# Relation products ahead of a block's sums, one-hots behind the messages, and an own order for the last set's products

## The reference, cut to what matters

```python
def _gat(x, W, asrc, adst, b, src, dst):
    h = (x @ W).reshape(n, HEADS, HID)                 # 4 heads of 64
    es = jnp.sum(h * asrc, axis=-1); ed = jnp.sum(h * adst, axis=-1)
    e = jax.nn.leaky_relu(es[src] + ed[dst], 0.2)
    emax = jax.ops.segment_max(e, dst, num_segments=n)
    ex = jnp.exp(e - emax[dst])
    den = jax.ops.segment_sum(ex, dst, num_segments=n)
    out = jax.ops.segment_sum(h[src] * (ex / den[dst])[:, :, None], dst, num_segments=n)
    return out.mean(axis=1) + b
# layer 1, layer 2, each with a layer norm and relu; then h @ Wo + bo, added to x, layer norm
# relational layer:
out = x @ W0
h = jnp.einsum('nd,rdo->rno', x, W)                    # 8 relations
msg = h[edge_type, src] * edge_weight[:, None]
out = (out + jax.ops.segment_sum(msg, dst, num_segments=num_nodes)) / deg[:, None]
```

## Time and profile before

| what | value |
|---|---|
| median of 3 runs | 3734.32 us (3734.08 to 3737.24) |
| the profiled execution, whole | 3735.32 us |
| its span in the profile | 3733.7 us |
| POOL busy | 1742.3 us (47%) |
| DVE busy | 2104.0 us (56%) |
| PE busy | 2435.0 us (65%) |
| ACT busy | 729.1 us (20%) |

### The profile page before, as it was taken

The page is one execution under the profiler, slowest core; times in us unless marked ns, Lnnn a source line. Parts: engine busy times, 40 slices in busy tenths (PEclk is TensorE's granted clock), DMA queues, the critical chain, the costliest instruction groups (busy, mean ns, idle before and its releaser), DMA issues.

```text
span 3733.7 us, 49457 instructions
## 1 busy us (share of the span) xinstructions
PE 2435.0 (65%) x14591; PEld 1745.1 (47%) x14592; DVE 2104.0 (56%) x5733; ACT 729.1 (20%) x1115; POOL 1742.3 (47%) x1837
## 2 busy tenths in 40 slices
PE   5879999999999945565535666662333344545556
PEld 3545666666666534444424444442323233444444
DVE  8985555555555636666646666662333233555555
ACT  5870000000000033322222333320000002222222
POOL 2220000000000067777747777725777776777771
PEclk9989999999999967777767777776666666677778
DMA  2000000000000064444434555532222223444441
GB/s 66 5 1 0 0 0 0 0 0 0 0 0 0 13 180 138 137 142 140 121 112 132 154 154 155 151 88 59 58 58 59 58 61 106 131 131 131 130 124 44
DMA packets 139378, 283.87 MB, mean 76 GB/s; under 512 B 35751, under 2 KB 79123, under 8 KB 139155
## 3 DMA queue, kind: packets, MB, share of 16 engines
q0 software_dynamic: 77760, 204.68, 19.9%
q1 hardware_dynamic: 24603, 53.25, 4.3%
q10 hardware_dynamic: 36864, 24.07, 2.2%
HBM read 255.10 MB, written 27.01 MB: 76 GB/s over the span
## 4 chain that ended last, share of the span: by engine, by line
POOL 31%; issue 11%; DVE 10%; PE 10%; DMA 2%; ACT 1%; ACTq 0%; POOLq 0%; DVEq 0%
POOL t_rows L1833 11%; POOL t_rows L2176 11%; POOL t_rows L2497 9%; PE t_sum_ps L1930 5%; DVE t_onehot L1761 2%; PE t_product_ps L1650 1%; DVE t_rows L2009 1%; DVE t_stage L2577 1%; PE t_sum_ps L2548 1%; DMA t_rows<-gat_table,t_src 1%; DMA t_rows<-kv_table_b,t_src 1%; DVE t_stage L2572 1%; PE t_small_ps L1900 0%; DVE t_so_far L1984 0%; ACT t_stage L1687 0%
## 5 line engine op out<-in xcount | busy, mean ns | idle before, releaser
L1038 PE MATMUL hop_ps<-parts,counts 128*128 128x384 bf16 (+1 forms) x6150 | 1003.3, 326 | 2.2 <-DVE parts L1099 2.2
L1833 POOL DMA_INDIRECT t_rows<-gat_table,t_src x880 | 838.4, 953 | 323.2 <-issue 264.1
L1038 PEld LDWEIGHTS hop_ps<-parts,counts 128*128 (+1 forms) x6150 | 603.4, 98 | 402.2 <-issue 10.2
L1930 PE MATMUL t_sum_ps<-t_rows,t_onehot 128*128 128x264 f32 x1760 | 511.3, 460 | 229.1 <-DVE t_rows L2009 229.0
L1930 PEld LDWEIGHTS t_sum_ps<-t_rows,t_onehot 128*128 128x128 f32 x1760 | 404.1, 233 | 319.8 <-issue 213.7
L2176 POOL DMA_INDIRECT t_rows<-rel_table_b,t_rel x440 | 417.9, 950 | 211.6 <-issue 133.2
L2497 POOL DMA_INDIRECT t_rows<-kv_table_b,t_src x440 | 416.4, 946 | 153.0 <-issue 131.9
L1464 POOL IOTA t_node<- 128x1 f32 x1 | 0.1, 131 | 1044.6 <-POOLq L106 1044.6
L2194 PE MATMUL t_sum_ps<-t_rows,t_onehot 128*128 128x128 f32 x880 | 159.1, 365 | 332.9 <-DMA t_rows<-rel_table_b,t_rel 332.9
L2194 PEld LDWEIGHTS t_sum_ps<-t_rows,t_onehot 128*128 128x128 f32 x880 | 155.1, 278 | 341.2 <-issue 341.2
L2527 PE MATMUL t_small_ps<-t_own,t_turned 128*128 128x128 bf16 x1032 | 118.5, 311 | 246.0 <-DVE t_stage L2572 240.4
(11 more groups left out here) (351 smaller groups left out, 2873.0 us busy)
## 6 DMA issues: line engine op xcount, KB each, us to landing
t_dst_wide<-dst_row SPq DMA_DIRECT2D x72, 576.0 KB, 4.3
t_rows<-gat_table,t_src POOLq DMA_INDIRECT x880
rel_table_b<-t_stage ACTq DMA_DIRECT2D x25, 512.0 KB, 3.6
t_rows<-rel_table_b,t_rel POOLq DMA_INDIRECT x440, 2.5
t_rows<-kv_table_b,t_src POOLq DMA_INDIRECT x440, 2.7
gat_table<-t_own ACTq DMA_DIRECT2D x10, 520.0 KB, 4.7
kv_table_b<-t_fresh ACTq DMA_DIRECT2D x5, 512.0 KB, 3.0
out<-x SPq DMA_DIRECT2D x6, 256.0 KB
```

The lines of the kernel that those rows point to most:

```text
L1038: last = nc.tensor.matmul(ps[bank][0:m, 0:PARTS * D], counts[:, k, columns], parts[old][:, k, :], start=(k == 0), stop=(k == NB - 1))
L1833: c.nc.gpsimd.indirect_dma_start(t.rows[:, slot(k), 0:FW], None, self.table, bass.IndirectOffsetOnAxis(ap=t.src[:, k:k + 1], axis=0)).then ...
L1930: product = c.nc.tensor.matmul(t.pa[b % 2][:, 0:RW], t.onehot[:, hot_at(k), :], t.rows[:, slot(k), :], start=(n == 0), stop=(n == len(ks) ...
```

## The change

Four edits:

1. **PE and ACT, in each block of both layers' loop:** `late(b)`, the relation products of two blocks, stands before the block's own sums on PE (behind `look_up`), and on ACT directly behind the block's exponentials, before `own_weight` and `turn`. Behind layer 1 `late` does nothing.
2. **DVE, both layers:** `make_hots(b + 1)` moves from before `messages(b)` to behind `close(b - 1)` and the norm, and `view(b + 1)` moves with it, ahead of `self.after.dve`. For block 23 (y) the one-hots of block 24 move behind `close(x)`.
3. **The last set's products** (`pe_last`, `act_last`, `dve_last`): the 512-column products of a block go to PSUM bank 0 and 1, ACT copies the first half out and DVE the second, and the DMA of the block goes out after both. The three W0 products (128 columns) follow after all six halves.
4. **Relational layer:** since the last W0 products are copied out late, PE waits for them before its first sums (`own_out`), and DVE before it closes block 22.

No instruction is added or taken away but for three copies that change engine, three DMAs that stay on ACT, and waits.

```diff
--- before.py
+++ after.py
@@ -1603,6 +1603,15 @@
     def act_late(self, act, i, blocks):
         pass
 
+    def pe_last(self, pe):
+        pass
+
+    def act_last(self, act):
+        pass
+
+    def dve_last(self, dve):
+        pass
+
     def dve(self, dve, layer, i):
         dve.wait_ge(self.out, SETS[i][-1] + 1)
         then = chained(dve, self.step, 4 * i)
@@ -1619,6 +1628,7 @@
         self.early, self.late = 0, 0
         self.turned, self.copied, self.done, self.added, self.normed, self.step, self.x_turned, self.x_copied, self.x_done, self.x_out = (
             c.sem(f"into_rel_{n}") for n in ("turned", "copied", "products", "added", "normed", "step", "x_turned", "x_copied", "x_products", "x_out"))
+        self.x_out_dve = c.sem("into_rel_x_out_dve")
         self.tabled = [c.sem(f"into_rel_tabled{q}") for q in range(3)]
 
     def pe(self, pe, layer, i):
@@ -1648,6 +1658,54 @@
                 if k >= 2:
                     pe.wait_ge(self.x_out, k - 1)
                 c.nc.tensor.matmul(t.pr[k % 2][:, 0:(hi - lo) * D], t.turned_all[:, j * P:(j + 1) * P], t.w_rel[:, lo:hi, :], start=True, stop=True).then_inc(self.x_done, 1)
+
+    def pe_last(self, pe):
+        c, t, blocks = self.c, self.t, SETS[-1]
+        n, k0 = len(blocks), 3 * blocks[0]
+        self.pe_turn(pe, len(SETS) - 1)
+        for j in range(n):
+            columns = t.turned_all[:, j * P:(j + 1) * P]
+            pe.wait_ge(self.x_out, k0 + j - (j == 0))
+            c.nc.tensor.matmul(t.pr[0][:, 0:4 * D], columns, t.w_rel[:, 0:4, :], start=True, stop=True).then_inc(self.x_done, 1)
+            if j:
+                pe.wait_ge(self.x_out_dve, j)
+            else:
+                pe.wait_ge(self.x_out, k0)
+            c.nc.tensor.matmul(t.pr[1][:, 0:4 * D], columns, t.w_rel[:, 4:NREL, :], start=True, stop=True).then_inc(self.x_done, 1)
+        for j in range(n):
+            if j % 2:
+                pe.wait_ge(self.x_out_dve, n)
+            else:
+                pe.wait_ge(self.x_out, k0 + n + j // 2)
+            c.nc.tensor.matmul(t.pr[j % 2][:, 0:D], t.turned_all[:, j * P:(j + 1) * P], t.w_rel[:, NREL, :], start=True, stop=True).then_inc(self.x_done, 1)
+
+    def act_last(self, act):
+        c, t, blocks = self.c, self.t, SETS[-1]
+        n, k0, m = len(blocks), 3 * blocks[0], len(blocks) * P
+        act.wait_ge(self.x_turned, len(SETS))
+        act.wait_ge(self.x_done, k0)
+        c.nc.scalar.copy(t.turned_all[:, 0:m], t.pt[:, 0:m]).then_inc(self.x_copied, 1)
+        rows = self.table.rearrange("(r n) f -> n r f", r=NREL)
+        for j, b in enumerate(blocks):
+            act.wait_ge(self.tabled[b % 3], 16 * (b // 3))
+            act.wait_ge(self.x_done, k0 + 2 * j + 1)
+            c.nc.scalar.copy(t.stage[:, b % 3, 0:4 * D], t.pr[0][:, 0:4 * D]).then_inc(self.x_out, 1)
+            act.wait_ge(self.x_out, k0 + j + 1)
+            act.wait_ge(self.x_out_dve, j + 1)
+            act.dma_start(rows[b * P:(b + 1) * P, :, :], t.stage[:, b % 3, :].rearrange("p (r f) -> p r f", r=NREL)).then_inc(self.tabled[b % 3], 16)
+        for j, b in enumerate(blocks):
+            act.wait_ge(self.x_done, k0 + 2 * n + j + 1)
+            c.nc.scalar.copy(t.own[:, b, 0:D], t.pr[j % 2][:, 0:D]).then_inc(self.x_out, 1)
+
+    def dve_last(self, dve):
+        t, blocks = self.t, SETS[-1]
+        for j, b in enumerate(blocks):
+            dve.wait_ge(self.tabled[b % 3], 16 * (b // 3))
+            dve.wait_ge(self.x_done, 3 * blocks[0] + 2 * j + 2)
+            self.c.nc.vector.tensor_copy(t.stage[:, b % 3, 4 * D:NREL * D], t.pr[1][:, 0:4 * D]).then_inc(self.x_out_dve, 1)
+
+    def own_products_out(self):
+        return self.x_out, 3 * SETS[-1][0] + 2 * len(SETS[-1])
 
     def pe_turn(self, pe, i):
         c, t, blocks = self.c, self.t, SETS[i]
@@ -1870,12 +1928,12 @@
         for b in range(NB - 2):
             keep(b)
             exponentials(b)
+            late(b)
             if b:
                 own_weight(b - 1)
             self.turn(act, b + 2)
             if b - 1 in SET_DONE:
                 self.after.act(act, self, SET_DONE[b - 1])
-            late(b)
         keep(NB - 2)
         exponentials(NB - 2)
         own_weight(NB - 3)
@@ -1885,7 +1943,7 @@
         own_weight(NB - 1)
         late(NB - 1)
         self.after.act(act, self, len(SETS) - 1)
-        late(NB)
+        self.after.act_last(act)
 
     def pe(self, pe):
         c, t = self.c, self.t
@@ -1959,7 +2017,7 @@
         add_up(z, 0, len(tiles_of(z)))
         late(z)
         self.after.pe(pe, self, len(SETS) - 1)
-        late(NB)
+        self.after.pe_last(pe)
 
     def dve(self, dve, enter=None):
         c, t, v = self.c, self.t, self.c.nc.vector
@@ -2043,23 +2101,24 @@
                 at_nodes(b - 1)
             raise_(b)
             weigh(b)
-            make_hots(b + 1)
             messages(b)
             if b:
                 close(b - 1)
             if b - 1 in SET_DONE:
                 norm(SET_DONE[b - 1])
+            make_hots(b + 1)
+            view(b + 1)
+            if b - 1 in SET_DONE:
                 self.after.dve(dve, self, SET_DONE[b - 1])
-            view(b + 1)
             if b == 1 and enter is not None:
                 enter.dve_late(dve)
         x, y, z = NB - 3, NB - 2, NB - 1
         at_nodes(x)
         raise_(y)
         weigh(y)
-        make_hots(z)
         messages(y)
         close(x)
+        make_hots(z)
         view(z)
         raise_(z)
         weigh(z)
@@ -2070,6 +2129,7 @@
         close(z)
         norm(len(SETS) - 1)
         self.after.dve(dve, self, len(SETS) - 1)
+        self.after.dve_last(dve)
 
 
 def pieces_of(blocks):
@@ -2180,8 +2240,9 @@
         for i in range(len(SETS)):
             self.after.act(act, self, i)
 
-    def pe(self, pe):
+    def pe(self, pe, own_out):
         c, t = self.c, self.t
+        pe.wait_ge(*own_out)
         for b in range(NB):
             if b - 1 in SET_DONE:
                 self.after.pe(pe, self, SET_DONE[b - 1])
@@ -2196,7 +2257,7 @@
                     product.then_inc(self.summed, 1)
         self.after.pe(pe, self, len(SETS) - 1)
 
-    def dve(self, dve):
+    def dve(self, dve, own_out):
         c, t, v = self.c, self.t, self.c.nc.vector
         then = chained(dve, self.step)
 
@@ -2209,6 +2270,8 @@
 
         def close(b):
             dve.wait_ge(self.summed, sums_through(b))
+            if b == SETS[-1][0]:
+                dve.wait_ge(*own_out)
             total = t.own[:, b, 0:D]
             v.tensor_tensor(total, total, t.pa[b % 2][:, 0:D], ALU.add).then_inc(self.freed, 1)
             dve.wait_ge(self.freed, b + 1)
@@ -2674,7 +2737,7 @@
                 enter.pe(pe)
                 first.pe(pe)
                 second.pe(pe)
-                relations.pe(pe)
+                relations.pe(pe, leave.own_products_out())
                 cross.pe(pe)
                 last.pe(pe)
 
@@ -2685,7 +2748,7 @@
                 dve.wait_ge(enter.numbered, 1)
                 first.dve(dve, enter)
                 second.dve(dve)
-                relations.dve(dve)
+                relations.dve(dve, leave.own_products_out())
                 cross.dve(dve)
                 last.dve(dve)
 
```

## The result

The changed kernel takes 3703.41 us (median of 4 runs, 3700.88 to 3705.45) against 3735.78 us for the kernel before (median of 4, 3734.08 to 3738.68). The ratio is 0.9912, 95% interval 0.9895 to 0.9929: 32 us faster; 3704 was predicted. The two profiled executions took 3735.32 and 3705.45 us, 30 us apart; all rows of the two kernels come from these. On a second chip of the same sort it was 3707.64 against 3739.14, ratio 0.9919 (0.9906 to 0.9933). On three other chips the same kernel before takes about 4135 us.

What follows compares the result with a forecast made beforehand. Layer 2's blocks lagged their gathers, delaying the relational layer; the change would make gathers the bound. 28.7 + 1.3 + 0.3 = 30.3 us off 3735.3 gives 3705.0, or 3704.0 as median; range 3700 to 3709 (72%).

Steps and rivals of the forecast that it cites:

- the backlog: Layer 2's blocks fall behind their gathers by 5.2 us a set; at block 23 this had reached 30.9 us.
- block 23's mark: End of weigh in layer 2's block 23, where DVE began the one-hots: forecast at 2461.4 instead of 2490.13, 28.7 us earlier.
- The set of four blocks: Layer 2's work for four blocks, 95.5 us before, would take 80.2, under the 90.3 of their gathers.
- The prediction's own sign of being wrong: Layer 2: wrong if ACT's keep in blocks 17 to 20 never waits for a gather, or sums take well over 11 us.
- I add nothing: TensorE's clock in layer 2: products take the slow start, sums run fast; costed at zero, at the other end +1.8 per block.
- the rival: Layer 2's matmuls throttled to 1.2 GHz throughout because PE waits more: about 3790 us; slower by more was given 3%.
- The stalls costed at nothing: Product blocks: DVE's close stalls up to 4 us for own_weight, covered by PE's sums; uncovered, 1 to 2 us per block.
- The last set: Last set's products to the last DMA issue: 9.0 us instead of 10.3, 1.3 us less, bounds 0 and 2.
- Layer 1: End of layer 1: block 23's sums start 0.9 us earlier; 0.3 us gained in all, bounds -0.3 and +0.7.
- the first rival: Only one of the two moves works, yet gains 28.2 us in all, 3706; counted within the forecast's own range, 72%.
- The part of a backlog that stays: Layer 2's sets take 92 to 94 us, ending 8 to 15 us later: 3712 to 3719; 3709 to 3722 was given 19%.
- Slower: The whole kernel slower than before by more than 0.2% (7.5 us), reasoned from TensorE's low clock in layer 2; chance 3%.

Runs made afterwards that it cites:

- f2: Changed kernel with the relation products put back behind the block's sums, keeping the one-hots' move and the last set's order: 3713.69 us, ratio 0.9933.
- f3: Kernel before with only the products moved ahead of the sums, on a chip of the predicted sort: 3709.97 us, ratio 0.9924.
- f1: Changed kernel again without an edit, against the kernel before on a second chip of the predicted sort: 3707.64 us, ratio 0.9919.
- f4: Changed kernel with layer 2's gathers fetching 520 bytes of a row instead of 1040: 3709.12 us, ratio 0.992.
- e3: Kernel before with only the last set's products in their new order, on a chip of the slower sort: 4134.52 us, ratio 0.999.
- e4: Kernel before with both moves but the last set's products as before, on a chip of the slower sort: 4172.94 us, ratio 1.0098.

## Why the prediction was right

The forecast's mechanism held, the work of a block falling under the pace of its gathers. That the sum came so near is in part luck, as the last paragraphs of this section show.

**What bounds it, and the backlog.** The step "block 23's mark: 2461.4 instead of 2490.13, so 28.7 us earlier" held. The mark stands at 2459.12, 31.0 earlier, 2.3 us more than forecast. That is the moment of 2459.2 which the prediction worked out for a block that isn't behind: the whole backlog is gone. ACT's timeline shows it: keep of block 22 waited 1.36 us for its last gather and that of block 23 5.96.

```profile
2422.87 0.58 ACT L1745 COPY t_stage<-t_product_ps 128x512 f32<-128x512 f32 x1 [0.22 <-PE t_product_ps L1660]
...
2424.12 0.21 ACT L1901 ACTIVATE t_own_w<-t_own_l 128x4 f32<-128x4 f32 x1 [0.50 <-ACT t_own L1745]
...
2431.14 0.25 ACT L1915 COPY t_es<-t_rows 128x72 f32<-128x72 f32 x1 [1.36 <-DMA t_rows<-gat_table,t_src]
...
2454.13 0.25 ACT L1915 COPY t_es<-t_rows 128x72 f32<-128x72 f32 x1 [5.96 <-DMA t_rows<-gat_table,t_src]
```

The set of four blocks was forecast at 80.2 of work under 90.3 of gathers. The marks of blocks 20, 21 and 22 were forecast at 2391.4, 2416.4 and 2437.0 and came at 2390.5, 2415.8 and 2435.4. The prediction's own sign of being wrong stayed away: keep in blocks 17 to 20 waited 3.40, 1.20, 6.07 and 11.51 us for gathers.

**The mis-sized term: sums behind products.** "Products take the slow start and the sums run fast. I add nothing" was right in its mechanism, but "I add nothing" was not what it comes to, since the cycle was reckoned with sums of 10 to 11 us. PE's timeline, blocks 20 (no products), 21 and 22:

```profile
2392.07 10.06 PE L1988 MATMUL t_sum_ps<-t_rows,t_onehot 128*128 128x264 f32 x36 [2.60 <-DVE t_rows L2067]
...
2416.80 3.60 PE L1660 MATMUL t_product_ps<-t_w_rel,t_turned_all 128*128 128x512 f32 x6 [1.11 <-ACT t_turned_all L1736]
2420.85 2.34 PE L1660 MATMUL t_product_ps<-t_w_rel,t_turned_all 128*128 128x512 f32 x6 [0.45 <-ACT t_stage L1745]
2423.03 8.18 PE L1988 MATMUL t_sum_ps<-t_rows,t_onehot 128*128 128x264 f32 x36
...
2436.34 2.83 PE L1660 MATMUL t_product_ps<-t_w_rel,t_turned_all 128*128 128x128 f32 x8 [0.26 <-ACT t_stage L1745]
2439.00 8.18 PE L1988 MATMUL t_sum_ps<-t_rows,t_onehot 128*128 128x264 f32 x36
```

Behind products the sums start with no wait and take 8.18 us, behind a pause 10.06. In block 21 they start 7.2 us after the mark, where 6.0 was forecast, because the first six passes of products take 3.60 us and not 2.34; but they end 15.4 after it and not at 16 or 17. From mark to mark that is 19.6 us for the 20.6 forecast. Of the 2.3 us by which the forecast missed block 23's mark, 0.9 stand already in block 20's, 1.0 come from this cycle and 0.6 from the next, and 0.3 are lost in between. Windows show why; the number behind the five engines' busy times is the granted clock. In the changed kernel it is 0.81 over block 20's sums and 1.00 over block 21's:

```profile
2392.00:2402.00 10.00, 9.93 (x36) 8.01 (x36) 9.38 (x32) 4.48 (x3) 7.56 (x9) 0.81 0.50 134
2423.00:2431.00 8.00, 8.00 (x38) 6.68 (x36) 5.21 (x10) 6.22 (x9) 6.08 (x7) 1.00 0.76 214
3629.00:3637.00 8.00, 6.76 (x36) 6.59 (x36) 5.73 (x13) 0.26 (x1) 0.05 (x1) 0.64 0.09 20
```

In the kernel before, the sums of block 22 begin at 2467.28 behind 4.83 us of idling, and their first 6 us run at 0.50; in the changed kernel it is the first products of block 21 that run at 0.50, and the sums no longer do. Three windows of before, one of after:

```profile
2467.30:2469.30 2.00, 2.00 (x5) 1.59 (x6) 2.00 (x3) 0.10 (x1) 0.00 (x0) 0.50 0.45 143
2471.30:2473.30 2.00, 2.00 (x6) 1.51 (x5) 1.84 (x6) 0.00 (x0) 0.00 (x0) 0.50 0.57 166
2473.30:2476.00 2.70, 2.70 (x14) 2.31 (x13) 2.31 (x15) 0.00 (x0) 0.00 (x0) 0.99 0.28 105
```

```profile
2416.80:2418.80 2.00, 2.00 (x3) 0.97 (x4) 2.00 (x3) 0.00 (x0) 1.67 (x2) 0.50 0.43 100
```

Over both layers the sums fell to 484.7 us, from 511.3, and PE's idling before them to 100.2, from 229.1:

```profile
L1988 PE MATMUL t_sum_ps<-t_rows,t_onehot 128*128 128x264 f32 x1760 | 484.7, 442 | 100.2 <-DVE t_rows L2067 100.1
```

That is why block 22's work ended early enough for the gathers to bound it. f2 and f3 separate the two moves: with products ahead 8.25 us for a block's sums, without them 10.4 to 11.0; over both layers 489.8 and 507.7. The rule of the Trainium skill's "TensorE: Matmul & The Clock Gate", "Part 1: The HAM clock gate" (throttled by default, released by activity), agrees with these rows, 0.50 behind a pause and 1.00 later. It worked for the change: the rival took it that PE would wait more, and the move filled pauses instead of making them.

**The stalls costed at nothing.** DVE's timeline, block 21: messages, close, one-hots, own_logit.

```profile
2416.26 5.28 DVE L2067 TENSOR_TENSOR t_rows<-t_rows,t_sum_ps 128x768 f32<-128x768 f32 x6 [0.31 <-ACT t_sum_ps L1921]
2424.36 0.16 DVE L2079 TENSOR_TENSOR t_rden<-t_sum_ps,t_own_w 128x4 f32<-128x4 f32 x1 [2.82 <-ACT t_own_w L1901]
...
2427.34 2.69 DVE L1819 TENSOR_TENSOR t_onehot<-t_small_ps,t_dst 128x768 f32<-128x768 f32 x3
...
2431.24 0.22 DVE L2073 SCALAR_TENSOR_TENSOR t_own_l<-t_sum_ps,alone,t_own_e 128x4 f32<-128x4 f32 x1 [0.70 <-PE t_sum_ps L1988]
```

Messages start 0.31 us behind the exponentials, close waits 2.82 us for own_weight, which stands behind the copies at 2424.12 (up to 4 were forecast), and the one-hots and view behind it end before PE's sums do: DVE then still waits 0.70 for them. The cover held, with 0.70 us to spare; it is the same in blocks 17 and 18.

**The last set.** All pieces in order of time, its first half, last copy and last issue:

```profile
2494.80 2.07 PE L1669 MATMUL t_product_ps<-t_w_rel,t_turned_all 128*128 128x512 f32 x2 [0.57 <-ACT t_turned_all L1687]
...
2502.53 0.69 DVE L1705 COPY t_stage<-t_product_ps 128x512 f32<-128x512 f32 x1 [1.30 <-PE t_product_ps L1674]
...
2503.31 0.37 ACTq L1695 DMA_DIRECT2D rel_table_b<-t_stage  x1
```

From 2494.80 to 2503.31 it is 8.51 us; 9.0 was forecast and 10.33 was before. So 1.8 us instead of 1.3.

**Layer 1.** Of "0.3 us" nothing is seen in the total: its last gather to layer 2's first takes 34.16 us, 1.0 more than before. Block 23's last gather, which is on the chain, landed in 4.11 us where it had taken 2.78:

```profile
1866.77 4.11 DMA t_rows<-gat_table,t_src
```

Less this landing, the stretch is 30.38 us in the kernel before and 30.48 in f3, which has the one-hots in their old place, but 30.05 in the changed kernel and 30.00, 30.12 and 29.91 in f1, f2 and f4, where they are moved. So the 0.3 us is there, and a longer landing covers it. What lengthens the landing is not settled. The store of set 5's table is issued at 1866.20, 0.6 us ahead of that gather and 2.5 us earlier than before; but in f1 it also comes first (by 0.8 us) and the landing takes 3.00, in f2 both fall together and it takes 4.09, in f4 likewise and it takes 3.45.

**What was given back.** From the first relational gather to the end the changed kernel takes 1196.5 us, 3.1 more than before (1193.4). 2.3 of these lie behind the last gather: block 23's sums in the transformer layer took 6.8 us (chain of the changed kernel) where the kernel before had 4.41:

```profile
3629.97 6.78 PE t_sum_ps L2611 x36
```

The row of the windows above for 3629 to 3637 gives a clock of 0.64. It goes with neither move: with the changed kernel's order f4 takes 4.41 us there and f1 6.75, with one move each f2 takes 4.41 and f3 6.82. What decides their length was not found.

**The sum.** Forecast: 28.7 for block 23's mark, 1.3 for the last set and 0.3 for layer 1, 30.3 in all. Measured: the mark 31.0 (0.8 of it because this execution's gathers of layer 2 ended 0.8 us earlier), the last set 1.8, and 0.3 between the mark and the last set's first product. That is 33.1 us up to the first relational gather; layer 1 adds nothing, for layer 2 starts 0.1 us later than before. Behind it 3.1 us are lost, which leaves 30.0 of the span. So the way to the relational layer was forecast 2.8 us too short, and a loss that the forecast did not have took the same away again: the mechanism is the forecast's, the agreement to a microsecond is luck.

**The rivals.** That each move alone would bring nearly the whole gain was the first rival, at 28.2: f2 and f3 brought 25.5 and 29.2 us of median. The part of a backlog that stays did not occur. Slower came true on another sort of chip, but by a mechanism that the prediction did not have: not the clock (its mean over the run is 0.767 in e3 and in e4), but the ring, which the earlier trace rows shows to be slack only on the chip where it was read.

## What to carry to other kernels

Compare what a block's work takes with what its transfers take: where two edits each bring the work below that pace, the second is worth next to nothing, and only the pace itself is left to shorten. Matmuls that can be moved are well placed in a pause of TensorE right ahead of its long burst: they take the low clock at the start of it, and the burst runs at the high one. Where a ring that sets the pace is freed by the end of that burst, the same move costs more than it saves. A trace shows the bounds of one chip: an edit that lengthens the way to a buffer's release should be priced for the case that the buffer does become the bound. Of the versions run, the one-hots' move is the one that gained on both sorts (0.9943 alone, and 0.9933 with the order of the last set).

## What was not expected of the hardware

One program took 3735.78 and 3739.14 us on two chips and 4132.23 to 4138.32, 11% more, on three. The first 1324 us are alike; the stages of gathers are 12 to 20% longer (layer 2 654 for 551 us, the transformer layer's stream 659 for 549), with TensorE making single passes 2.8 us apart for stretches. Halving the bytes of a gathered row changed nothing (3709.12 to 3707.64): POOL issued one gather of 128 rows in 1.25 us either way. The same 36 passes took 8.18 us behind other matmuls and 10 to 11 behind a pause.
